# Centring matrices by TensorE products, sums of squares on ScalarE, and a deeper pipeline in the key pass

## The reference

```python
def _layernorm(x, axis=-1, eps=1e-05):
    m = jnp.mean(x, axis=axis, keepdims=True)
    v = jnp.var(x, axis=axis, keepdims=True)
    return (x - m) / jnp.sqrt(v + eps)
...
x = x + _layernorm(_L0_attn_ref(_layernorm(x), ...))   # x1: a scan over time, y = (h*C) @ Wout.T + Dp*x
x = x + _layernorm(_L0_ffn_ref(_layernorm(x), ...))    # x2: 8 experts, each takes its 512 best tokens, output matrix W2
x = x + _layernorm(_L1_attn_ref(_layernorm(x), ...))   # x3: 8 heads, second-order Taylor attention, output matrix w_out
x = x + _layernorm(_L1_ffn_ref(_layernorm(x), ...))    # 8 experts, 2 per token, output matrix Wd
```

## Time and profile before

| what | us |
| --- | --- |
| median of 3 runs | 702.16 (701.15 to 703.88) |
| the profiled execution, its own time | 703.21 |
| its span, first to last instruction | 701.4 |

### The profile page before, as it was taken

How to read it: one execution, slowest core, us unless ns; L and a number is a source line. 1 busy time by engine, 2 the same in 40 slices (tenths; PEclk the granted TensorE clock), 3 DMA queues, 4 the chain that set the end, 5 groups by cost and what they waited for, 6 DMA issues and landing times.

```text
span 701.4 us, 13529 instructions
## 1 busy us (share of the span) xinstructions
PE 514.5 (73%) x3846; PEld 374.3 (53%) x3847; DVE 421.7 (60%) x1761; ACT 343.0 (49%) x724; POOL 310.7 (44%) x329
## 2 busy tenths in 40 slices
PE   1759521588758157878899994169999999999924
PEld 1447110356435023434334432159999999999911
DVE  4789768654312279897246878964455455545456
ACT  3815533344323034444357662246666666666525
POOL 3514300358878433342002112036676776667444
PEclk9976855599987569888899997569999999999966
DMA  7501263112333421100001010011111111111164
GB/s 187 138 0 48 79 274 147 28 41 44 42 47 39 100 100 32 32 0 1 1 1 31 16 31 21 24 22 48 46 49 45 49 49 45 49 43 52 35 230 141
DMA packets 47287, 42.22 MB, mean 60 GB/s; under 512 B 15345, under 2 KB 41322, under 8 KB 46730
## 3 DMA queue, kind: packets, MB, share of 16 engines
q1 hardware_dynamic: 31658, 25.35, 11.3%
q0 software_dynamic: 10368, 15.82, 10.1%
q10 hardware_dynamic: 5216, 0.52, 0.5%
HBM read 26.23 MB, written 15.30 MB: 59 GB/s over the span
## 4 chain that ended last, share of the span: by engine, by line
PE 48%; DVE 26%; issue 10%; POOL 6%; ACT 6%; DMA 3%; ACTq 1%; DVEq 0%; POOLq 0%; SPq 0%
PE bank L1916 18%; PE banks L1937 4%; PE bank L1937 4%; POOL sum_dram L683 3%; DVE st L1284 3%; PE bank L1774 3%; PE bank L1764 2%; PE bank L1729 2%; POOL arena L667 2%; DVE mv L1289 2%; DVE st L1014 2%; ACT arena L938 1%; POOL rstd L700 1%; PE bank L1830 1%; DVE hit L1147 1%
## 5 line engine op out<-in xcount | busy, mean ns | idle before, releaser
L1916 PE MATMUL bank<-arena 128*128 128x128 f32 x1136 | 140.9, 278 | 0.4 <-ACT arena L989 0.4
L1916 PEld LDWEIGHTS bank<-arena 128*128 128x128 f32 x1136 | 134.7, 195 | 0.7 <-ACT arena L989 0.7
L700 POOL TENSOR_TENSOR rstd<-ve,mhalf 128x4 f32<-128x4 f32 x40 | 48.8, 1219 | 167.6 <-DVE ve L1292 119.4
L1546 DVE TENSOR_TENSOR arena<-arena,bank 128x512 f32<-128x512 f32 x71 | 48.8, 688 | 82.4 <-PE bank L1916 82.4
L754 POOL DMA_INDIRECT y_dram<-arena,sidx x71 | 69.9, 985 | 44.9 <-DVE arena L1551 41.3
L975 ACT ACTIVATE arena<-wgu 128x1024 f32 x71 | 74.9, 1057 | 26.8 <-PE bank L1916 26.4
L746 POOL DMA_INDIRECT arena<-x3row_dram,gidx x71 | 68.8, 969 | 36.4 <-issue 21.0
L981 ACT ACTIVATE arena<-bank 128x512 f32<-128x512 f32 x71 | 42.4, 597 | 43.0 <-PE bank L1916 43.0
L667 POOL DMA_INDIRECT arena<-x1row_dram,idx x32 | 31.3, 979 | 43.8 <-DVE idx L1244 34.3
L683 POOL DMA_INDIRECT sum_dram<-arena,idx x28 | 44.2, 1577 | 10.9 <-issue 7.9
L1265 DVE TENSOR_TENSOR arena<-arena,bank 128x256 f32<-128x256 f32 x32 | 13.5, 422 | 57.3 <-ACT arena L870 57.3
(11 more groups left out here) (370 smaller groups left out, 1077.0 us busy)
## 6 DMA issues: line engine op xcount, KB each, us to landing
wgu<-in_wgu SPq DMA_DIRECT2D x1, 4096.0 KB, 12.4
wgu<-y_dram SPq DMA_DIRECT2D x8, 512.0 KB, 7.2
X<-in_x SPq DMA_DIRECT2D x8, 256.0 KB, 6.4
sum_dram<-zero POOLq DMA_DIRECT2D x8, 256.0 KB, 4.2
x1row_dram<-row SPq DMA_DIRECT2D x8, 256.0 KB, 2.4
w<-in_w SPq DMA_DIRECT2D x1, 2048.0 KB, 17.3
acc<-sum_dram SPq DMA_DIRECT2D x8, 256.0 KB, 2.9
w<-in_wd SPq DMA_DIRECT2D x1, 2048.0 KB, 9.9
```

The lines of the kernel that those rows point to most:

```text
L700: nc.gpsimd.tensor_tensor(out, ve[:, u], mhalf[:, 0:J], ALU.pow).then_inc(done, 1)
L1546: nc.vector.tensor_tensor(gl[:, m.pair], sgl[:, m.pair], bank[3 + m.pair][:], ALU.mult).then_inc(f_gated, 1)
L1916: last = nc.tensor.matmul(bank[first + m.pair][:, h * P:(h + 1) * P], wnow[:, m.pair, at_:at_ + P], xrT[:, m.ring], start=True, stop=True)
```

## The change

1. **Centring.** The output matrices are centred over the output features, so that each sublayer's output has mean zero: `wout` and `diagD` by VectorE before the scan; `w2` and `wd` by PE products with `centring` = identity - 1/128 (w2 in search rounds 4 to 11, `wd` in the steps of tiles 17 to 32 of the first experts), each evicted from PSUM by ScalarE; `wo` by VectorE after the first experts. `w2` and `wd` are loaded in another layout into the arena, ahead of `wgu`; the load of `wd` in the key pass goes.
2. **Sums of squares on ScalarE.** In the key pass (expert sums), in the last stage and for x3 of the last group, VectorE's `stats1` goes. ScalarE squares each tile with an accumulated sum (`squares_of`, four instructions a group), POOL adds EPS and takes the power (`power_of_squares`).
3. **The residual keeps its mean.** `mu`, the mean of the input, stands for the mean of x3; all instructions on `shift1` and `shift2` go.
4. **The last stage** applies factor and addition in one VectorE instruction a tile (four a group, instead of four on ScalarE and one on VectorE).
5. **The key pass is deeper.** ScalarE squares three groups ahead, VectorE updates X two ahead and makes the shift one ahead; normalising moves ahead of `evict(1)` on ScalarE; the transposes move ahead of the query product on PE.

```diff
@@ SP
             sp.wait_ge(a_scst, LEAD + SCORES * CH)
+            sp.dma_start(w2_in, inp["w2"]).then_inc(s_w2, 16)
+            sp.dma_start(w13[:], inp["w13"]).then_inc(s_w0, 16)
+            sp.dma_start(wd_in, inp["wd"]).then_inc(s_w0, 16)
             sp.dma_start(wgu[:], inp["wgu"]).then_inc(s_w1, 16)
-            sp.dma_start(w13[:], inp["w13"]).then_inc(s_w0, 16)
-            sp.dma_start(w2[:], inp["w2"]).then_inc(s_w0, 16)
...
-                    if early(g, 2) and g.b:
-                        sp.dma_start(wd, inp["wd"]).then_inc(s_w1, 16)
@@ POOL
+            def power_of_squares(out, u, wait, n, done):
+                pool.wait_ge(wait, LEAD + n)
+                pc.mark(nc.gpsimd.tensor_tensor(fv[:, u], fv[:, u], eps[:], ALU.add))
+                pc.wait()
+                nc.gpsimd.tensor_tensor(out, fv[:, u], mhalf[:, 0:J], ALU.pow).then_inc(done, 1)
...
             def key_pass(at):
-                h, g, m, l = at(2), at(1), at(0), at(-1)
+                h, g, m, l = at(3), at(2), at(0), at(-1)
                 if l:
                     logits_of_x2(l, slice(3, 4), d_lgx)
+                if h:
+                    if not early(h, 2):
+                        pool.wait_ge(d_x2, LEAD + h.n - 1)
+                    power_of_squares(frstd[:, h.b], h.b, d_fvar, h.n + 1, d_frstd)
+                if m:
+                    logits_of_x2(m, slice(0, 3), d_lgx)
                 if g:
...
                     power(rstd[:, g.b], g.b, d_xvar, g.n + 1, d_xrstd)
-                if h:
...
-                if m:
-                    logits_of_x2(m, slice(0, 3), d_lgx)
@@ ScalarE, search and first experts
+                f = (r - 6) // 2
+                if r % 2 == 0 and 0 <= f < 4:
+                    act.wait_ge(c_tot, LEAD + r + 1)
+                    nc.scalar.activation(w2[:, 2 * f:2 * f + 2].rearrange("p e h d -> p (e h d)"), bank[(1, 5)[f % 2]][:], ACT.Copy)
...
                     nc.scalar.activation(gT[:, o.pair], bank[4 + o.pair][:, 0:H0], ACT.Copy).then_inc(c_gt, 1)
+                    centred_wd(o.n)
@@ ScalarE, key pass
+            def squares_of(src, out, u, done, bias=None):
+                for j in range(J):
+                    last = nc.scalar.activation(out[:, u, j], src(j), ACT.Square, scale=float(D) ** -0.5,
+                                                bias=0.0 if bias is None else bias[:, j:j + 1], accum_out=fv[:, u, j:j + 1])
+                last.then_inc(done, 1)
...
                 evict(0)
+                if g:
+                    act.wait_ge(d_xnmr, LEAD + g.n + 1)
...
+                    normalise(lambda j: xn[:, g.b, j], tokens(g), g.b).then_inc(d_xn, 1)
+                if h:
+                    act.wait_ge(d_acc[h.b], LEAD + 16 * h.trip + 16)
...
+                    squares_of(lambda j: acc[:, h.b, j], row, h.b, d_fvar)
                 evict(1)
                 evict(2)
+                if g:
+                    act.wait_ge(d_xtps, LEAD + g.n + 1)
...
+                    nc.scalar.activation(xnT[:, g.b], bank[0][:], ACT.Copy).then_inc(d_xt, 1)
...
+            groups(act, key_pass, 3, 0, 1)
@@ VectorE
+            do(nc.vector.tensor_reduce(wsum[:], wout[:], AX.X, ALU.add))
+            for b in range(NB):
+                nc.vector.scalar_tensor_tensor(wout[:, b], wsum[:, b:b + 1].to_broadcast([P, P]), -1.0 / D, wout[:, b], ALU.mult,
+                                               ALU.add)
             dve.wait_ge(a_dt, LEAD + CH)
...
             def key_pass(at):
-                h, g, m = at(2), at(1), at(0)
+                g, f, m = at(2), at(1), at(0)
...
                     for j in range(J):
...
                     last.then_inc(d_x2, 1)
+                if f:
+                    shift(f.b, d_xrstd, f.n + 1, d_xnmr)
                 key_products(m, 0)
...
-                if h:
-                    dve.wait_ge(d_acc[h.b], LEAD + 16 * h.trip + 16)
...
-                    stats1(lambda j: acc[:, h.b, j], h.b, d_fvar)
-                if g:
-                    shift(g.b, d_xrstd, g.n + 1, d_xnmr)
...
-                ch.mark(nc.vector.scalar_tensor_tensor(nmr[:, m.b], mv[:, m.b, :, 0], -1.0, rstd[:, m.b], ALU.mult, ALU.mult))
-                ch.wait()
-                do(nc.vector.tensor_tensor(shift1[:, m.place], nmr[:, m.b], shift1[:, m.place], ALU.add))
-                nc.vector.tensor_tensor(shift2[:, m.place], shift1[:, m.place], shift2[:, m.place], ALU.add)
...
-            x3_stats(end)
...
                 if l:
-                    dve.wait_ge(g_out, LEAD + l.n + 1)
-                    x = xl[:, l.place].rearrange("p j d -> p (j d)")
-                    nc.vector.tensor_tensor(x, x, (ysum[:, l.n, 0] if l.n < BY_DVE else bank[l.n])[:, 0:W], ALU.add).then_inc(g_x, 1)
+                    dve.wait_ge(g_rstd, LEAD + l.n + 1)
+                    for j in range(J):
+                        last = nc.vector.scalar_tensor_tensor(
...
+                            rstd[:, l.b, j:j + 1], xl[:, l.place, j], ALU.mult, ALU.add)
@@ PE
+                if 4 <= r < 12:
+                    if r == 4:
+                        pe.wait_ge(s_w2, LEAD + 16)
+                    for k in range(2 * (r - 4), 2 * (r - 3)):
+                        nc.tensor.matmul(bank[(1, 5)[k // 4 % 2]][:, k % 4 * P:(k % 4 + 1) * P], w2_in[:, k], centring[:],
...
+                    for q in range(2):
+                        last = nc.tensor.matmul(bank[4 + n % 2][:, H0 + q * P:H0 + (q + 1) * P], wd_in[:, e, 2 * half + q], centring[:],
```

More of the change, by code:

```diff
@@ L878, in _ @@
             straight(T, move0, 1, 1)
+            for n in range(T, FIRST_WD + 2 * E1):
+                act.wait_ge(c_gtps, LEAD + n + 1)
+                centred_wd(n)
             def normalise(out, src, b):
@@ L999, in finish @@
                 g = at(0)
-                act.wait_ge(g_nmr, LEAD + g.n + 1)
-                for j in range(J):
-                    y = (ysum[:, g.n, 0] if g.n < BY_DVE else bank[g.n])[:, j * P:(j + 1) * P]
-                    last = nc.scalar.activation(y, y, ACT.Identity, bias=nmr[:, g.b, j:j + 1], scale=rstd[:, g.b, j:j + 1])
-                last.then_inc(g_out, 1)
+                if g.n < BY_DVE:
+                    act.wait_ge(g_add, LEAD + g.n + 1)
+                else:
+                    act.wait_ge(g_sum, LEAD + g.n - BY_DVE + 1)
+                at_least(act, g_rstd, g.n - 1)
+                squares_of(lambda j: (ysum[:, g.n, 0] if g.n < BY_DVE else bank[g.n])[:, j * P:(j + 1) * P], row, g.b, g_var)
             each_group(finish, 0)
@@ L1750, in _ @@
             straight(T, experts0, 1, 2)
+            for n in range(T, FIRST_WD + 2 * E1):
+                pe.wait_ge(c_gt, LEAD + min(n, T))
+                centre_wd(n).then_inc(c_gtps, 1)
             pe.wait_ge(d_scaled, LEAD + 1)
+            pe.wait_ge(s_wc, LEAD + 1)
             for b in range(NB):
@@ L1784, in key_pass @@
                 qkv(2)
+                if g:
+                    pe.wait_ge(d_xn, LEAD + g.n + 1)
+                    if not early(g, 1):
+                        pe.wait_ge(d_xt, LEAD + g.n)
+                    for j in range(J):
+                        last = nc.tensor.transpose(bank[0][:, j * P:(j + 1) * P], xn[:, g.b, j], ident[:])
+                    last.then_inc(d_xtps, 1)
                 if m:
```

152 lines of the change are left out of this document (79 added, 73 removed).

## The result

The changed kernel takes **682.81 us** (median of 4 runs, 679.94 to 683.49), the kernel before 702.39 beside it: ratio 0.9713, 95% interval 0.9678 to 0.9747. The profiled execution took 683.49 us, with a span of 681.7 us (before: 703.21 and 701.4). The forecast was 683.9, with a range of 679.5 to 691.0.

The account below looks back on a forecast made before the run. It took different bounds by stage, in the key pass VectorE's work plus a round trip through ScalarE's eviction; terms summed to -18.8 from 703.21, 684.4, or 683.4 as a median; it said 683.9, range 679.5 to 691.0.

Parts of the forecast that it names:

- Key pass, -15.3: Key pass: turns of 8.5 us (8.1 to 9.2) instead of 10.52, last group's first product at 312.6 instead of 327.92.
- a square with its sum: ScalarE in the key pass: 0.37 to 0.50 us a square, 1.5 to 2.0 a group, 1.5 taken.
- PE's clock: Key pass: PE has less idle time in a turn, so its granted clock falls less, over 0.80.
- Centring `wout`, +1.0: Before the scan: one reduction and two instructions on VectorE cost their own time, +1.0 us (0.8 to 1.3).
- x1 stage, -0.6: x1 stage: eight shift2 instructions go from busy VectorE, each worth 0.08 us, -0.6 in all.
- Search +0.1, first experts 0: Centring products on PE and evictions on ScalarE: +0.1 us in the search, hidden under POOL's scatters in the first experts.
- Query pass and lists, -0.2 - 0.4 - 1.4: Small shift instructions go: -0.2 us in the query pass, -0.4 after its last group; x3's last statistics leave VectorE: -1.4.
- Last stage, -2.0: Last stage: VectorE's statistics go, inputs arrive no earlier; end at 699.35 instead of 701.40, -2.0 us.
- (a): Rival: ScalarE's order becomes the bound, squares at 0.6 us or PE at half clock, turns about 10; about 691; chance 0.11.
- (b): Rival: running POOL instructions keep VectorE out of SBUF, about 2.4 us a key pass turn; about 699; chance 0.03.
- (c): Rival: slower than before, squares with a sum on ScalarE far dearer; at 1.03 us each about 710; chance 0.03.
- (d): Rival: key pass still follows the round trip, turn near 10, only VectorE's wait grows; about 696; chance 0.05.

Follow-up runs that it names:

- e4: The changed kernel with VectorE computing the middle group's shift before the update of X in a key pass turn, not after; 681.12 us.
- e5: e4 with the centring of wout moved into VectorE's wait for PE before the parts of the third chunk; 680.37 us.
- e3: The changed kernel with four more, unused squares with a sum on ScalarE in each group of the key pass; 690.24 us.
- e8: e4 with one more, unused power on GpSimd (POOL) in each turn of the key pass; 683.51 us.
- e7: e5 with PE's first wqkv product ahead of accumulating key product 2, and one small instruction fewer ending the x2 statistics; 678.99 us.
- e11: The changed kernel with the last stage's variance computed by VectorE statistics instead of ScalarE squares, outputs still centred; 685.89 us.
- e1: The changed kernel with the key pass steps in the old order, no deeper than before, squares still on ScalarE; 696.45 us.

## Why the prediction was right, point by point

- **Key pass, -15.3.** Measured -16.6 in the middle and +0.1 ahead of it. The turn of 8.37 lies in the 8.1 to 9.2 given (taken: 8.5), the wait is where it was said to be, before the second product and naming the eviction, and the last group's first product came at 312.22 (312.6 + 0.5 forecast). Term by term, from the first group's first product on: 3.2 for 3.7, 33.5 for the four turns of 8.5, 8.0 for 8.1, 6.5 for 6.5, and 5.0 for 4.4. The first product was to be 0.7 late; it came 0.1 later after the last scatter in this profile and 0.8 in e4's.
- **The mis-sized term: a square with its sum.** The forecast had 0.37 to 0.50 us and 1.5 to 2.0 a group. It is 0.29 and 1.17. What the read adds was right, 0.09 a square (283.04 to 283.13). The error is in what it was added to: I took the copy's duration of 0.28, but in a row of instructions the next one starts before the one ahead has ended. The earlier trace rows shows it, a duration of 0.34 and the next start after 0.23 (317.33, 317.56), and in the changed kernel a copy of 136 columns is followed after 0.16 (284.22, 284.38). So it should have been a distance of some 0.2 (the square's own is 0.20) plus 0.09.
- **The step that was missing.** ScalarE's chain was counted from PE: product, accumulation, `evict(0)`. In the trace ScalarE waits for the shift instead. The two errors are of opposite sign, 4 x 0.08 or more too much for squares and 0.33 left out, and cancel nearly: that 8.5 was so near to 8.37 is luck to that extent. e4 shows the second alone.
- **PE's clock.** The forecast took a turn near the low end because PE would have less idle time and its clock would fall less. It did: 0.84 before and 0.98 now from the first to the last group's first product.
- **Centring `wout`, +1.0.** The three instructions take 0.86 of the path (36.87 to 37.73), and the scan is 0.58 later since the steps ahead happened to be 0.28 early. e5 confirms the term, at 0.86.
- **x1 stage, -0.6.** This profile shows +1.05, the wrong sign. Here are the products of x1 with `wg` and the whole stretch, first of the changed kernel, then of e4, which has the same code there:

```profile
78.87 3.58 PE L1680 MATMUL bank<-x1T,wg 128*8 128x512 f32 x4
...
76.00:92.00 16.00, 11.15 (x25) 3.43 (x25) 6.93 (x44) 7.92 (x17) 3.02 (x3) 0.57 0.24 69
```

```profile
79.02 2.78 PE L1680 MATMUL bank<-x1T,wg 128*8 128x512 f32 x4
...
76.00:92.00 16.00, 9.11 (x25) 3.17 (x25) 7.09 (x45) 8.08 (x17) 3.02 (x3) 0.76 0.25 71
```

  The same four products take 3.58 or 2.78 us, at a granted clock of 0.57 or 0.76 in the stretch. With 0.57 the stage is 52.5 to 52.6 us long (the changed kernel twice, e3, e8), with 0.64 to 0.71 it is 51.4 to 52.0 (the seven others), and with 0.76 it is 50.74 in e4 against 51.52 in the kernel before, which had 0.76 too. At equal clock the change gives -0.8, near the -0.6 forecast, and the rows of this pair show where: e4 starts the scan 0.74 behind the kernel before and is level with it by 78.7, mostly in steps of 0.06 to 0.09 at the updates of X, where the `shift2` instructions were. Of the 1.8 between e4 and the changed kernel, 1.7 come in PE's products with `wg`. What makes the chip grant the one or the other here stays open.
- **Search +0.1, first experts 0.** 39.92 against 39.91, and 103.1 to 104.4 over the profiles taken against 104.17: the centring by PE is free, hidden under POOL's scatters.
- **Query pass and lists, -0.2 - 0.4 - 1.4.** The query pass shows +0.6, but over the profiles of kernels with the same query pass it was 105.0 to 107.5 long; -0.2 can't be seen in that. Of the 1.8 in the lists 1.3 to 1.4 came. The small instructions brought 0.46 and the statistics 1.38, and then a new wait gave back 0.5:

```profile
446.10 0.23 DVE L1568 SCALAR_TENSOR_TENSOR sif<-bank,slot_pad 128x71 f32<-128x71 f32 x1 [0.49 <-PE bank L1957]
```

  In the kernel before this instruction followed the one ahead of it at once, since PE's one-hot products were done. What is late next was not asked at this place in the forecast. A second bound lies close by: in e5, e7 and e8 the stage, with the same code, took 22.4 to 22.9 us, and there POOL's first gather waits for the transfer to `x3row_dram`.
- **Last stage, -2.0.** Measured -2.35, an end 6.5 us after PE's last addition (the forecast's sum gives 6.8, its list of signs says 6.9): squares 1.29 with the latency to POOL (675.23 to 676.52), POOL 1.3, the update 1.1, the end 2.7. The terms fit; what the forecast did not see is that without the squares on ScalarE the stage would have lost (e11).
- **Rivals.** (a) fell with squares at 0.29 and turns of 8.37. (b) fell by the products, which last 1.21 to 1.24 beside POOL, also where POOL is first, as here in e4:

```profile
290.88 1.01 POOL L715 TENSOR_TENSOR frstd<-fv,mhalf 128x4 f32<-128x4 f32 x1
290.94 1.22 DVE L1384 TENSOR_TENSOR arena<-arena 128x1024 f32<-128x1024 f32 x1
```

  The power runs at its shortest here and the product at its usual length. Where the power begins inside a product, it ends 0.86 to 0.87 behind the product, in all 22 such cases of four profiles (before, changed, e4, e8); for those that begin early in the product, this makes the 1.9 to 2.1 us of which the earlier trace rows shows one. So the power isn't done before the product is, and POOL, whose operands are four columns, keeps VectorE out for 0.03 us at most: in e4 and e8 the first product behind the statistics starts 0.08 or 0.19 after the last small instruction where no power is running, and 0.08 or 0.21 where one is.

  The Trainium skill (SBUF — State Buffer, "Who interferes with whom") has it that the shared ports are an exclusive lock and that whoever issues first blocks the other. The trace agrees in one order (POOL waits for the product). In the other order no run here shows VectorE waiting for the power's 1.0 us, so the price of rival (b), 2.4 us a turn, is not there.

  (c) and (d) fell with the rows of the turn; e1 is what (d) would have looked like, 696.45 for the 696 given. Rival (c) had a turn of 6.4 + S with S for a group's squares. The turns of 8.37 (S = 1.17) and of 9.5 (S = 2.34, in e3) say 7.2 + S, so dear squares would have hurt sooner than it said.

The range of 679.5 to 691.0 held both medians, 682.81 and 681.58; of the ten executions of the changed kernel (678.46 to 683.71) two lie under it. The sum of the forecast gave 683.4, and the 0.5 that were added to it have no term. What the sum had wrong also cancelled in part: the key pass gained 1.2 more than forecast, the x1 stage lost 1.05 instead of gaining 0.6.

## What to carry to other kernels

A wait at the end of a round trip and a loaded engine are to be taken on together: lighter alone gave 1.2 us and deeper alone 10.0 where both gave 16.6 (between the first and the last group's first product), because lighter alone turned VectorE's work into waits, and deeper alone left VectorE full. When a step is moved to an in-order queue, look at what the steps behind it wait for in its new place, down to the smallest: here one shift of 0.15 us stood behind an update of 1.13 and cost 0.36 in every turn. And where an engine is nearly full, a cheaper form of one step can be a dearer form of another, as the scaled update in the last stage is while the statistics are on VectorE too (e11).

## What the runs showed of the hardware

- A square of 128 columns with its sum on ScalarE can follow the one before after 0.29 us: 0.20 for the square and 0.09 for the read of the sum, though the profile gives them durations of 0.29 and 0.19. A copy of 136 columns with a duration of 0.26 is followed after 0.16 (284.22 and 284.38). What an instruction adds to a full queue is the distance between starts and not its duration.
- GpSimd's power of 4 columns takes 1.0 us by itself, or when it starts 0.04 to 0.8 before a VectorE product of two operands in SBUF. Started inside such a product, it ends 0.86 to 0.87 behind the product's end, however much of the product was left. VectorE's product takes 1.21 to 1.24 in every case. An instruction on a queue of its own can therefore be twice as slow by where its start falls.
- PE's 16 accumulating products took 1.22 us at the lower granted clock and 0.71 at the full one. In the kernel before, the slow rows follow an idle time of PE of 2.24 us; in the steady turns of the changed kernel PE's longest idle time was 0.86 and the granted clock 1.00.
- The same code got a granted TensorE clock of 0.57 or 0.76 in one stretch, and the stage was 1.8 us longer with the lower one (52.57 and 50.74). Differences under 2 us between two profiles of this kernel have to be read at the instructions that the edit touches, not at the end of the span.
